# Expert stage of a gated cross-attention and MoE block: 64 experts of 96 slots against 48 tiles of 128 slots, with five scatter targets in DRAM

## The chip, the cores and the metric

The kernel runs on one core of one Trainium2 chip. The metric is the device time of one execution in microseconds; the median of three runs is given, and beside it the profile of one execution. A core has TensorE (matmuls, PE; its weight loads are listed apart as PEld), VectorE (DVE), ScalarE (ACT), GpSimd (POOL) and SyncE (SP, which here only issues transfers). A queue of transfers belongs to the engine that issues them (SPq, ACTq, POOLq); all queues are served by the same 16 DMA engines.

## The reference, cut to what matters

The block takes 16 sequences of 128 rows and 256 columns, 2048 tokens in all. It adds a cross-attention, and then a mixture of experts: 64 experts, six chosen for each token, 96 slots for each expert; every token beyond the 96th of an expert lands in its last slot, where only the last one written counts.

```
x = x + tanh(g_xattn) * xattn(layernorm(x), ctx)
logits = xn @ gate_weight.T; scores = softmax(logits)
topk_w, topk_i = top_k(scores kept in the 3 best groups, 6)
slot = expert * 96 + min(position in expert, 95)
buf = zeros(64 * 96, 256).at[slot].set(xn[tok])
g, u = buf @ Wg.T, buf @ Wu.T              # 176 columns for each expert
out = (silu(g) * u) @ Wd.T
y = sum over the 6 slots of a token of out[slot] * topk_w
x = x + tanh(g_ffn) * (y + shared(xn))     # shared: 352 columns
```

## The kernel before

All engines run a program written out by hand; semaphores order them. Everything is float32, but for the routing.

**Attention and routing** take eight steps, two sequences each (`step(r, h, par)` on each engine). In a step DVE normalises the rows into `xn2` (`norm2`, L1059), and SP saves them to `xn_rows` in DRAM (`saves`, L290), with the routing weights beside them (L297). There is one `xn2` buffer, so `norm2` of a step waits until the save of the step before has landed (`xn_saved`). DVE works out which token is in which slot; `slot_tables` turns this into two tables of row numbers, `gidx` for gathers and `sidx` for scatters. A shared expert (`shared_up`, `late_up`, `shared_down`) is computed on the way.

**SP's queue** begins with the loads of x, then the fills with zeros (L259, L262) of `even_rows`, `third_rows` and the pads behind the tables, then the experts' weights. `load_weights(g)` loads a group of two experts (1056 KB) into a ring of 12 groups; it waits until group g-2 has landed, and for g of 12 and over until the experts that used the place are done (`o_done`). The saves of `xn2` are issued on this queue, between groups: the first save follows group 3.

**The expert stage** runs over 64 experts, one after the other. POOL gathers the 96 rows of an expert with an indirect DMA (`gather`, L1540), six experts ahead. PE turns them (`turn_rows`, L582: two transposes), multiplies them by the two up projections (`up`: 8 matmuls, the weights stationary, 96 columns moving), ACT and DVE form silu(g) * u (L898, L1407), and PE multiplies by the down projection (`down`: 2 matmuls, the activations stationary, 256 columns of weights moving). One float32 matmul shows as two records on PE and two on PEld, a transpose as one of each. PE's order is `turn_rows(e+1)`, `up(e)`, `down(e-1)`. ACT scales the result by the slot's weight into `outs` (`take_out`, L909) and POOL adds it to one of three targets in DRAM with an indirect DMA that accumulates (`add_up`, L1548). Expert e goes to target e mod 3, and waits until the scatter of e-3 has landed. The third target is the output itself, which holds x and the shared expert's part from saves during the steps (`save_y`).

**The tail.** When the scatters have landed, SP reads the two other targets back (L321), PE has put the contributions of the crowded last slots into PSUM (`ov_done`), DVE adds the three (L1478, L1481), and POOL adds the sum to the output in four transfers that accumulate (L1575).

## Time and profile before

| what | value |
|---|---|
| median of 3 runs | 437.4 us (434.9 to 438.97) |
| the profiled execution | 439.52 us |
| its span on the core | 437.8 us |
| PE busy | 342.1 us, 78% |
| DVE busy | 215.8 us, 49% |
| POOL busy | 176.3 us, 40% |
| moved by DMA | 70.50 MB |

The span runs from the first to the last instruction of the profiled execution. Shares of busy time are means over stages with different limits: the steps take the first 200 us or so, the expert stage the next 205, the tail the last 30. The granted clock is TensorE's, as a share of 2.4 GHz.

### The profile page before, as it was taken

Reading aid. Unit: us, or ns where it says so; the run is one execution under the profiler, and the core shown is the slowest. Engines: PE = TensorE matmul, PEld = TensorE weight load, DVE = VectorE, ACT = ScalarE, POOL = GpSimd, SP = SyncE. Lnnn points to the kernel's source line nnn. Section 1 sums busy time; section 2 is a strip of 40 time slices with the busy share of each in tenths; the row PEclk is TensorE's granted clock in tenths of the full one; section 3 lists DMA queues with packets and bytes.
Section 4 is the critical chain, followed back from the end, with each engine's and each line's share of the span. In section 5 each row is a group of like instructions: output and inputs, shape, how many; then the busy total and the mean of one; then the engine's idle time right before and its main releaser. Section 6 shows DMA issues by size and latency. Waiting matters only on the chain.

```text
span 437.8 us, 8616 instructions
## 1 busy us (share of the span) xinstructions
PE 342.1 (78%) x2589; PEld 286.3 (65%) x2589; DVE 215.8 (49%) x879; ACT 155.8 (36%) x464; POOL 176.3 (40%) x173
## 2 busy tenths in 40 slices
PE   2779598998999796998987888777968897878600
PEld 1667486876887674886866676666856775767400
DVE  5656568789588888344764111211111211157390
ACT  2566355675466311111423223322323423223000
POOL 3000011010100111022577777776777777776231
PEclk9999979999899999899999899998999999989855
DMA  8798948447100111012598999898899444444797
GB/s 296 285 337 226 266 111 263 125 131 224 58 25 6 49 31 32 25 41 81 142 261 221 250 259 259 215 231 240 216 253 255 76 77 72 73 71 57 178 298 125
DMA packets 36265, 70.50 MB, mean 161 GB/s; under 512 B 6221, under 2 KB 23401, under 8 KB 36231
## 3 DMA queue, kind: packets, MB, share of 16 engines
q1 hardware_dynamic: 21851, 50.56, 37.0%
q0 software_dynamic: 12352, 16.26, 21.2%
q10 hardware_dynamic: 2028, 3.25, 2.3%
q8 instruction: 19, 0.31, 0.3%
q14 instruction: 15, 0.12, 0.1%
HBM read 52.26 MB, written 17.78 MB: 160 GB/s over the span
## 4 chain that ended last, share of the span: by engine, by line
PE 22%; issue 16%; DMA 8%; DVE 7%; POOL 7%; another core or an unknown queue 3%; ACT 2%; SPq 1%; DVEq 0%; ACTq 0%; POOLq 0%
PE bank L347 20%; DMA ctx_sb<-xn_rows,gidx 3%; PE bank L582 2%; DMA w_ring<-third_rows 2%; POOL result L1548 2%; POOL even_rows L1548 2%; DMA qk_sb<-xn_rows,gidx 2%; SPq L321 1%; DMA v_sb<-xn_rows,gidx 1%; POOL third_rows L1548 1%; POOL ctx_sb L1540 1%; DVE hi_hot L1188 1%; DMA even_rows<-x_all,sidx 1%; ACT pt_sb L898 1%
## 5 line engine op out<-in xcount | busy, mean ns | idle before, releaser
L347 PE MATMUL bank<-p_sb,w_ring 128*88 128x96 f32 x1024 | 97.6, 249 | 0.6 <-issue 0.6
L347 PEld LDWEIGHTS bank<-p_sb,w_ring 128*88 128x88 f32 x1024 | 92.0, 160 | 0.9 <-issue 0.8
L1407 DVE TENSOR_TENSOR pt_sb<-pt_sb,bank 88x192 f32<-88x192 f32 x64 | 22.4, 350 | 135.1 <-ACT pt_sb L898 76.4
L1529 POOL TENSOR_SCALAR zeros<-zeros,token 128x256 f16<-128x256 f16 x16 | 14.7, 928 | 155.4 <-DVE zeros L1197 155.4
L347 PE MATMUL bank<-d_ring,pt_sb 88*96 88x256 f32 x256 | 68.7, 392 | 9.5 <-DVE pt_sb L1407 9.5
L898 ACT ACTIVATE pt_sb<-bank 88x192 f32<-88x192 f32 x64 | 20.9, 327 | 94.2 <-PE bank L347 49.7
L347 PEld LDWEIGHTS bank<-d_ring,pt_sb 88*96 88x96 f32 x256 | 37.7, 167 | 19.2 <-DVE pt_sb L1407 11.7
L1548 POOL DMA_INDIRECT even_rows<-x_all,sidx x22 | 31.7, 1439 | 13.3 <-issue 4.9
L893 ACT ACTIVATE p_sb<-bank 128x192 f32<-128x192 f32 x64 | 21.1, 329 | 42.6 <-PE bank L582 22.9
L1548 POOL DMA_INDIRECT third_rows<-x_all,sidx x21 | 30.1, 1435 | 11.1 <-issue 4.0
L1548 POOL DMA_INDIRECT result<-x_all,sidx x21 | 30.2, 1436 | 10.5 <-issue 4.3
L1540 POOL DMA_INDIRECT qk_sb<-xn_rows,gidx x24 | 22.7, 947 | 24.9 <-DVE sidx L1361 17.9
L909 ACT ACTIVATE x_all<-bank,slot_w 96x256 f32<-96x256 f32 x64 | 29.6, 463 | 1.4 <-PE bank L347 0.7
L347 PE MATMUL bank<-xt_sb,sgu_sb 128*128 128x256 f32 (+1 forms) x96 | 24.2, 406 | 4.0 <-DVE x_all L1215 4.0
L347 PE MATMUL bank<-xt_late,sgu_sb 128*128 128x256 f32 (+1 forms) x96 | 23.4, 395 | 4.3 <-DVE act_t L1079 4.3
L347 PE MATMUL bank<-sd_sb,act_t 128*128 128x256 f32 (+1 forms) x96 | 25.5, 412 | 0.8 <-DVE x_all L1215 0.4
L1540 POOL DMA_INDIRECT ctx_sb<-xn_rows,gidx x24 | 22.4, 933 | 7.3 <-issue 5.5
L809 ACT ACTIVATE tanh_sb<-bank 128x256 f32<-128x256 f32 (+1 forms) x24 | 9.1, 384 | 41.2 <-PE bank L347 33.2
L347 PEld LDWEIGHTS bank<-xt_sb,sgu_sb 128*128 128x128 f32 (+1 forms) x96 | 17.9, 193 | 7.6 <-issue 4.4
L347 PE MATMUL bank<-qk_sb 128*128 128x256 f32 x64 | 18.4, 413 | 5.4 <-ACT p_sb L761 3.0
L347 PEld LDWEIGHTS bank<-xt_late,sgu_sb 128*128 128x128 f32 (+1 forms) x96 | 17.3, 186 | 8.0 <-issue 3.9
L347 PEld LDWEIGHTS bank<-sd_sb,act_t 128*128 128x128 f32 (+1 forms) x96 | 19.1, 207 | 3.8 <-DVE act_t L1079 0.7
(164 smaller groups left out, 593.6 us busy)
## 6 DMA issues: line engine op xcount, KB each, us to landing
w_ring<-wgu_in SPq DMA_DIRECT2D x32, 704.0 KB
d_ring<-wd_in SPq DMA_DIRECT2D x32, 352.0 KB
even_rows<-zeros SPq DMA_DIRECT2D x1, 2048.0 KB, 7.3
third_rows<-zeros SPq DMA_DIRECT2D x1, 2048.0 KB, 13.4
xn_rows<-xn SPq DMA_DIRECT2D x8, 256.0 KB, 5.0
result<-x_all SPq DMA_DIRECT2D x8, 256.0 KB, 2.2
w_ring<-even_rows SPq DMA_DIRECT2D x4, 512.0 KB, 7.0
w_ring<-third_rows SPq DMA_DIRECT2D x4, 512.0 KB, 7.9
```

Source lines behind the costliest of these rows:

```text
L321: sp.dma_start(rows_sb[:, n * q:n * (q + 1), :], d[P * n * q:P * n * (q + 1), :].rearrange("(n p) f -> p n f", p=P))\
L347: return pe.matmul(o, lhsT, rhs, start=start, stop=stop, skip_group_check=True)
L582: last = pe.transpose(t_ps[:, h * C:(h + 1) * C], rows[b % ROWS][:, h * P:(h + 1) * P], ident[0:C, 0:C])
L809: act.activation(tanh_sb[0:n, b, :], ps[m][0:n, 0:L], ACT.Tanh, scale=0.5)\
L893: act.activation(rows_t[:, b % 2, :], t_ps, ACT.Copy).then_inc(s["t_out"], 1)
L898: act.activation(silu_sb[:, b % 2, :], eg_ps[b % 2][:, 0:2 * C], ACT.Silu).then_inc(s["silu_ready"], 1)
L909: act.activation(outs[b % OUTS], o_ps[b % 2], ACT.Copy, scale=slot_w[:, b % 4:b % 4 + 1])\
L1188: last = dve.tensor_tensor(hi_hot[:, i, :].rearrange("p (k a j) -> p k a j", k=BLKS, a=HI), hi_key[:, i, :].rearrange("p (k a j) -> p k a ...
L1407: dve.tensor_tensor(act_tt[:, b % 2, :], silu_sb[:, b % 2, :], eg_ps[b % 2][:, 2 * C:4 * C], ALU.mult)\
L1529: last = pool.tensor_scalar(lo_hot[:, i, :], lo_hot[:, i, :], token1[:, at:at + 1], None, ALU.mult)
L1540: pool.indirect_dma_start(rows[e % ROWS], None, xn_dram, bass.IndirectOffsetOnAxis(ap=gidx[:, e:e + 1], axis=0))\
L1548: pool.indirect_dma_start(targets[e % 3], bass.IndirectOffsetOnAxis(ap=sidx[:, e:e + 1], axis=0), outs[e % OUTS], None, compute_op=ALU.add)\
```

## The change

The slots of four experts (384) are cut into three tiles of 128 slots, 48 tiles in all. Gathers, the transposes of the gathered rows, the scaling and the scatters are done by tile; `up` and `down` are still done by expert, on 96 columns of a window of six turned tiles. `down` now holds the weights stationary, in four matmuls of 96 moving columns, and its result is turned: DVE copies it out of PSUM (`take_ot`), and PE turns it back by tile (`turn_out`, two transposes). DVE forms the slot weights of three tiles at once (`slot_weights`), and copies the last slots (`keep_lasts`), which PE turns at the end; they no longer go through DRAM.

The scatters go to `acc_rows`, which holds five targets; expert e uses target e mod 5, so that a tile waits only for the scatter three tiles before. The output is no target any more: the saves of x during the steps are gone, x stays in SBUF (`outs` takes other buffers). All five targets are filled with zeros at the start, on SP's queue, at the place of the old fills. At the end the five are read back (three on SP's queue, two on ACT's); DVE adds four of them to x in SBUF in passes of eight, PE adds the fifth in PSUM, and SP writes the result with plain transfers. Token t is now kept at place (t mod 128) * 16 + t // 128 of the tables in DRAM, so that a partition's rows lie together.

```diff
+EB_TILES = EB * C // P
+TILES = E * C // P
+TARGETS = 5
+FILL_BY = 4
+TR = T + P
-AHEAD = 6
-ROWS = 8
-OUTS = 8
+AHEAD = 7
+ROW_BLKS = 3
+ROWS = ROW_BLKS * EB_TILES
+TURNED = 6
+OUTS = 4
+FILL = TR * L // P // FILL_BY
...
+            for k in range(TARGETS):
+                sp.dma_start(acc_dram.rearrange("(p a) f -> p (a f)", p=P)[:, k * FILL_BY * FILL:(k + 1) * FILL_BY * FILL]
+                             .rearrange("p (a f) -> p a f", a=FILL_BY), zero4).then_inc(s["fills_in"], 16)
+            sp.dma_start(xn_dram[T:TR, :], fill_zeros[:, 0:XW]).then_inc(s["fills_in"], 16)
...
+            read_back(sp, 4, TILES - 4)
+            read_back(sp, 0, TILES - 3)
+            read_back(sp, 2, TILES - 1)
+            for q in range(QUARTERS):
+                sp.wait_ge(s["sum_ready"], PAIRS // QUARTERS * (q + 1))
+                sp.dma_start(out_to[:, n * q:n * (q + 1), :], x_all[:, n * q:n * (q + 1), :]).then_inc(s["result_out"], 16)
...
+            def down(e):
+                at = e % (RING * GE) * DW
+                pe.wait_ge(s["at_out"], e + 1)
+                wait(pe, s["ot_out"], e - 1)
+                for h in range(H2):
+                    for m in range(2):
+                        last = mm(ot_ps[e % 2][:, h * C:(h + 1) * C],
+                                  d_ring[:, at + m * L + h * P:at + m * L + (h + 1) * P],
+                                  act_tt[:, e % 2, m * C:(m + 1) * C], start=m == 0, stop=m == 1)
+                last.then_inc(s["o_done"], 1)
+            def turn_out(t):
+                pe.wait_ge(s["ot_out"], last_expert(t) + 1)
+                wait(pe, s["o_ready"], t - 1)
+                for h in range(H2):
+                    last = pe.transpose(o_ps[t % 2][:, h * P:(h + 1) * P],
+                                        turned[t // EB_TILES % 2][:, h, P * (t % EB_TILES):P * (t % EB_TILES + 1)],
+                                        ident[:, :])
+                last.then_inc(s["turned_out"], 1)
...
+            for e in range(1, E):
+                multiply(e)
+                take_ot(e - 1)
+                if e % EB == 0:
+                    keep_lasts(e // EB - 1)
+                    slot_weights(e // EB)
+                if e % 3 == 2 and e // 3 < N:
+                    weight_parts(e // 3)
...
+            for r in range(PAIRS):
+                dve.wait_ge(s[f"back4_{r * QUARTERS // PAIRS}"], 16)
+                dve.tensor_tensor(pair(x_all, r), pair(x_all, r), pair(back[4], r), ALU.add).then_inc(s["added4"], 1)
...
+            for r in range(PAIRS):
+                dve.wait_ge(s[f"back3_{r * QUARTERS // PAIRS}"], 16)
+                dve.tensor_tensor(pair(x_all, r), pair(x_all, r), pair(back[3], r), ALU.add).then_inc(s["added3"], 1)
+                dve.wait_ge(s["ov_done"], r + 1)
+                dve.tensor_tensor(pair(x_all, r), pair(x_all, r), sum_ps[r][:, :], ALU.add).then_inc(s["sum_ready"], 1)
...
+            def add_up(t):
+                pool.wait_ge(s["o_ready"], t + 1)
+                if t > 2:
+                    pool.wait_ge(s[f"acc_in{(t - 3) % OUTS}"], 16 * ((t - 3) // OUTS + 1))
+                pool.indirect_dma_start(acc_dram, bass.IndirectOffsetOnAxis(ap=sidx[:, t:t + 1], axis=0),
+                                        outs[t % OUTS], None, compute_op=ALU.add)\
+                    .then_inc(s[f"acc_in{t % OUTS}"], 16)
```

SP's queue behind the loads of x, before. The first four groups of weights and the first save of `xn2` (L290) stand behind the fills.

```order
5 L259 DMA even_rows<-zeros 1024x1x512
6 L259 DMA third_rows<-zeros 1024x1x512
7 L262 DMA xn_rows<-zeros 96x320
8 L262 DMA even_rows<-zeros 96x256
9 L262 DMA third_rows<-zeros 96x256
10 L262 DMA result<-zeros 96x256
11 L276 DMA w_ring<-wgu_in 128x1408
12 L277 DMA d_ring<-wd_in 88x1024
...
19 L290 DMA xn_rows<-xn 128x2x256
```

The same place of the queue with the change.

```order
5 L295 DMA acc_rows<-w_ring 128x4x1088 x5
6 L297 DMA xn_rows<-w_ring 128x320
7 L311 DMA w_ring<-wgu_in 128x1408
8 L312 DMA d_ring<-wd_in 88x1024
...
15 L318 DMA xn_rows<-xn 128x2x256
```

The five fills write 4 * 1088 * 4 bytes in each of 128 partitions, 2.23 MB each, 11.14 MB in all, and the pad of `xn_rows` 0.16 MB. Before it was 2 * 2.10 MB and pads of 0.42 MB: 4.61 MB. What follows them is in the same order as before, up to the saves of x, which are gone.

PE in the middle of the expert stage, before: an expert is two transposes of gathered rows, `up` and `down`.

```order
209 L582 MATMUL bank<-ident,qk_sb 128x96 x2
210 L347 MATMUL bank<-p_sb,w_ring 88x96 x8
211 L347 MATMUL bank<-d_ring,pt_sb 96x256 x2
212 L582 MATMUL bank<-ident,qk_sb 128x96 x2
213 L347 MATMUL bank<-p_sb,w_ring 88x96 x8
214 L347 MATMUL bank<-d_ring,pt_sb 96x256 x2
```

PE with the change, over four experts (L609 is `turn_rows`, L643 `turn_out`; in L375, `hi_hot,w_ring` is `up` and `xn,d_ring` is `down`).

```order
219 L609 MATMUL bank<-ident,ctx_sb 128x128 x2
220 L375 MATMUL bank<-hi_hot,w_ring 88x96 x8
221 L375 MATMUL bank<-xn,d_ring 128x96 x4
222 L643 MATMUL bank<-ident,act_t 128x128 x2
223 L375 MATMUL bank<-hi_hot,w_ring 88x96 x8
224 L375 MATMUL bank<-xn,d_ring 128x96 x4
225 L609 MATMUL bank<-ident,p_sb 128x128 x2
226 L375 MATMUL bank<-hi_hot,w_ring 88x96 x8
227 L375 MATMUL bank<-xn,d_ring 128x96 x4
228 L643 MATMUL bank<-ident,pt_sb 128x128 x2
229 L609 MATMUL bank<-ident,p_sb 128x128 x2
```

A `down` has four matmuls where it had two, and two transposes of results stand behind it wherever a tile is full: 96 transposes of rows and 96 of results over the stage, where there were 128 of rows.

DVE at the end of its program, before: these pairs of adds stand eight times, one pair for two sequences.

```order
547 L1478 TENSOR_TENSOR w_ring<-w_ring 128x512
548 L1481 TENSOR_TENSOR w_ring<-w_ring,bank0 128x512
549 L1478 TENSOR_TENSOR w_ring<-w_ring 128x512
550 L1481 TENSOR_TENSOR w_ring<-w_ring,bank1 128x512
551 L1478 TENSOR_TENSOR w_ring<-w_ring 128x512
```

DVE at the same place with the change; the last two stand eight times in turn.

```order
657 L1521 TENSOR_TENSOR x_all<-x_all,w_ring 128x512 x8
658 L1525 TENSOR_TENSOR x_all<-x_all,w_ring 128x512 x8
659 L1529 TENSOR_TENSOR x_all<-x_all,w_ring 128x512 x8
660 L1533 TENSOR_TENSOR x_all<-x_all,w_ring 128x512
661 L1536 TENSOR_TENSOR x_all<-x_all,bank2 128x512
```

The adds go from 16 to 40, and the first three passes must be through before the first quarter of the result can be complete.

## Rows read from the trace of the kernel before

**Rows 1.** Windows: the expert stage (us, busy by engine, PEclk, DMA share, GB/s)

```profile
210.00:404.00 194.00, 160.08 (x1370) 135.23 (x1368) 55.61 (x208) 61.65 (x186) 142.33 (x120) 0.97 0.75 181
```

**Rows 2.** Timeline of POOL: the first scatter, and a steady stretch

```profile
213.26 1.52 POOL L1548 DMA_INDIRECT even_rows<-x_all,sidx  x1 [3.16 <-ACT x_all L909]
...
323.24 0.94 POOL L1540 DMA_INDIRECT qk_sb<-xn_rows,gidx  x1 [0.30 <-DVE slot_w L1416]
324.48 1.44 POOL L1548 DMA_INDIRECT third_rows<-x_all,sidx  x1 [0.30 <-issue]
```

**Rows 3.** The scatters' line L1548: what POOL waited for (us, times)

```profile
  ACT x_all L909: 11.5, 11
  DVE slot_w L1416: 10.1, 9
  DMA even_rows<-x_all,sidx: 0.3, 1
```

**Rows 4.** Timeline of PE: one expert that waits for nothing

```profile
329.95 0.33 PE L582 MATMUL bank<-ident,qk_sb 96*128 96x96 f32 x2
...
330.12 1.49 PE L347 MATMUL bank<-p_sb,w_ring 128*88 128x96 f32 x16
...
331.44 1.03 PE L347 MATMUL bank<-d_ring,pt_sb 88*96 88x256 f32 x4
...
332.31 0.33 PE L582 MATMUL bank<-ident,qk_sb 96*128 96x96 f32 x2
```

**Rows 5.** Timeline of PE: 128 stationary columns, in a step

```profile
103.11 0.60 PE L383 MATMUL bank<-ident,p_sb 128*128 128x128 f32 x4
103.54 0.61 PE L347 MATMUL bank<-qkv_sb,ctx_sb 128*128 128x128 f32 x4
...
107.44 1.10 PE L347 MATMUL bank<-gate_sb,xt_sb 128*128 128x64 f32 x8 [0.25 <-ACT xt_sb L787]
```

**Rows 6.** Timeline of SP's queue: first fill, group 2, first save

```profile
14.36 0.61 SPq L259 DMA_DIRECT2D even_rows<-zeros  x1
...
36.21 0.36 SPq L276 DMA_DIRECT2D w_ring<-wgu_in  x1
...
42.54 0.40 SPq L290 DMA_DIRECT2D xn_rows<-xn  x1
```

**Rows 7.** Timeline of DVE: the second pair's norm

```profile
52.12 0.81 DVE L1059 TENSOR_SCALAR xn<-x_all,mv,guess 128x256 f32 x2 [4.45 <-DMA xn_rows<-xn]
```

**Rows 8.** Windows of the start (columns as in rows 1)

```profile
5.00:10.00 5.00, 1.47 (x4) 1.18 (x4) 4.28 (x28) 2.48 (x5) 0.53 (x3) 1.00 1.02 397
...
20.00:25.00 5.00, 3.96 (x26) 2.81 (x24) 1.74 (x5) 3.85 (x13) 0.00 (x0) 1.00 1.02 351
```

**Rows 9.** Timeline of PE: `down` of expert 0, and of the last

```profile
209.66 1.10 PE L347 MATMUL bank<-d_ring,pt_sb 88*96 88x256 f32 x4 [0.25 <-DVE pt_sb L1407]
...
401.58 2.11 PE L347 MATMUL bank<-d_ring,pt_sb 88*96 88x256 f32 x8
```

**Rows 10.** Timeline of POOL and SP's queue: last scatter, reads, last write

```profile
406.16 1.43 POOL L1548 DMA_INDIRECT even_rows<-x_all,sidx  x1 [0.30 <-issue]
...
427.12 1.28 POOL L1575 DMA_DIRECT2D result<-w_ring  x1 [1.73 <-DVE w_ring L1481]
...
409.47 0.42 SPq L321 DMA_DIRECT2D w_ring<-even_rows  x1
```

**Rows 11.** Windows of the tail: reading back, accumulating writes

```profile
417.00:419.00 2.00, 0.00 (x0) 0.00 (x0) 1.64 (x4) 0.00 (x0) 0.00 (x0) 0.74 1.09 348
...
427.00:429.00 2.00, 0.00 (x0) 0.00 (x0) 0.00 (x0) 0.00 (x0) 1.28 (x1) 0.50 1.24 196
```

**Rows 12.** Groups by line: DVE's adds; and transfers to landing

```profile
L1478 DVE TENSOR_TENSOR w_ring<-w_ring 128x512 f32<-128x512 f32 x8 | 5.5, 688 | 7.1 <-DMA w_ring<-third_rows 7.1
...
result<-x_all SPq DMA_DIRECT2D x8, 256.0 KB, 2.2
```

**Rows 13.** Chain that ended last: a gather's transfer (start, us)

```profile
320.26 6.67 DMA qk_sb<-xn_rows,gidx
```

More of the change, by code:

```diff
@@ L235, in build @@
[L235 to L242 removed]
+            rows_in0 rows_in1 rows_in2 rows_in3 rows_in4 rows_in5 rows_in6 rows_in7 rows_in8
@@ L695, in _ @@
-            for t in range(N):
-                pe.wait_ge(s["w_parts_ready"], t + 1)
-                if t // 2 == 6:
-                    pe.wait_ge(s["o_ready"], E)
-                for k, part in enumerate((high_mid, high_mid, high_low)):
-                    if k == 0 and t in early:
-                        continue
-                    last = mm(bank[t // 2][:, t % 2 * L:(t % 2 + 1) * L], part[:, t * P:(t + 1) * P],
-                              last_parts[:, k, :], start=k == 0, stop=k == 2)
-                last.then_inc(s["ov_done"], 1)
+            turn_rows(1)
@@ new lines, in _ @@
+            take_rows(0)
+            act.wait_ge(s["ht_done"], N)
+            silu(0)
+            take_rows(1)
+            act.wait_ge(s["qk_done"], N)
+            act.wait_ge(s["h_done"], N)
+            for e in range(1, E):
+                if e < E - 1 and last_tile(e + 1) > last_tile(e):
+                    take_rows(last_tile(e + 1))
+                silu(e)
+                t = last_tile(e - 2) if e > 1 else 0
+                if last_expert(t) == e - 2:
+                    take_out(t)
+                elif t > 0 and last_expert(t - 1) == e - 2:
+                    take_out(t - 1)
@@ L1530, in weigh_hots @@
                 last.then_inc(s["hot_ready"], 1)
[L1532 to L1533 removed]
+            for r in range(2, PAIRS + 1):
                 weigh_hots(r)
[L1536 to L1542 removed]
@@ L1544, in add_up @@
[L1544 to L1551 removed]
+            pool.wait_ge(s["qk_done"], N)
+            pool.wait_ge(s["v_done"], N)
```

544 lines of the change are left out of this document (285 added, 259 removed).

## Prediction, made blind

> **What bounds the kernel now.** I read the windows first. In the expert stage, 210 to 404 us, PE is busy 160.08 of 194 us, POOL 142.33, DVE and ACT about 60, and the DMA engines 0.75 [rows 1]. None is full, so the next view is POOL's timeline. There gather and scatter alternate with 0.30 us between them: 0.94 + 0.30 + 1.44 + 0.30 = 2.98 us for an expert, 191 us for 64, near to the stage's length. The gaps are the engine's own, not a wait [rows 2]. The scatters' own view shows how much POOL waited beyond that: 11.5 + 10.1 us for ACT and DVE, which is mostly where the rows of a gather had come late, and 0.3 us for an earlier scatter [rows 3]. So POOL's number of instructions sets the pace. PE is second: where an expert waits for nothing, it takes 2.36 us from one turning of rows to the next (329.95 to 332.31), 151 us for 64 [rows 4].
>
> Ahead of the stage the steps are bound by PE and DVE in turn, but at one place by a transfer. SP issues the fills from 14.36 us; group 2 of the weights must wait until group 0, behind the fills, has landed (36.21), group 3 waits in the same way for group 1, and only then goes the first save of `xn2` at 42.54 [rows 6]. DVE's second norm waits for that save, 4.45 us, until 52.12 [rows 7]. While the fills run the DMA engines are full, at 351 GB/s [rows 8]. So what stands ahead of this save on SP's queue is on the path.
>
> **The change: the expert stage.** POOL has 48 gathers and 48 scatters for 64 of each, but of 128 rows for 96. No row shows another number of rows. If a DMA costs the same whatever its rows, a tile takes 2.98 us; if it goes with the rows, 1.25 + 0.30 + 1.92 + 0.30 = 3.77 us. I take 1.03 and 1.57 us, near the lower end, since the direct transfers at the end issue 512 rows of 1 KB in 1.28 us [rows 10]. From the first scatter on there are 48 scatters and 41 gathers: 48 * 1.87 + 41 * 1.33 = 144 us, with 137 and 170 at the ends. Before it was 194 us from 213.26 to 407.6.
>
> The Trainium skill (DMA: Bandwidth & Descriptors, Anatomy of one DMA) says of descriptor generation that many descriptors can be emitted before the incremental cost shows up; by it the lower end holds, 137 us, and the sum stays as it is, for PE is then the bound either way.
>
> PE loses nothing but gains transposes. From 209.66 us (`down` of expert 0 [rows 9]) there are 62 `up` left, each 331.44 - 330.12 = 1.32 us: 82 us. `down` was four records with 256 moving columns, 332.31 - 331.44 = 0.87 us [rows 4]. Now it is eight records with 96 moving columns and 128 stationary ones. Rows with 128 stationary columns show what that costs: eight with only 64 moving columns are 1.10 us on PE, of which 0.17 us is the last one's way out (as with `up`, 1.49 us long at a pace of 1.32), so 0.93 us [rows 5]. The loads set that pace, not the moving columns. `up` has 88 stationary columns and goes at 0.083 us a record; at that pace `down` would be 0.66 us. I take 0.94, from the row with the same load: 64 of them are 60 us. Four transposes of 128 columns follow each other in 103.54 - 103.11 = 0.43 us [rows 5], 0.22 us for a tile; 45 tiles of rows and 48 of results are left: 20.5 us. Sum 163 us. TensorE's granted clock was 0.97 of full in this stage [rows 1], which adds 5 us; PE will be denser, so I don't take less. For rows that come late I add 4 us: the DMA engines have the same bytes to move in less time, and DVE's `slot_weights` wants three tiles landed before the next `multiply`. PE then ends its last `down` 172 us after 209.66, where it took 194.0 (to 401.58 + 2.11 [rows 9]): **22 us saved**, between 30 and 10.
>
> The Trainium skill (TensorE: Matmul & The Clock Gate, LDWEIGHTS) says that a weight load takes its number of columns divided by 1.2 in ns, whatever the contraction. By it eight loads of 128 columns are an estimated 0.85 us, 5.5 us less in all than by the row, and the sum would be 439.5. The rule too speaks against stationary weights here; of the trace, the transposes agree with it and the eight matmuls don't, so it is a rival below.
>
> DVE gets `take_ot` beside `multiply`, of the same size; it was busy 55.61 of 194 us [rows 1], and twice that still fits in 172. It is hidden by PE's 2.6 us for an expert; if that cover went, it would be POOL's pace that shows. The five targets change no wait that exists: three scatters were in flight before, and POOL waited 0.3 us for them [rows 3]. The old saves of x and the wait for them are gone; they held the seventh gather, but not PE, so I count nothing.
>
> **The start.** Fills and pads grow from 4.61 to 11.30 MB and stand ahead of group 0, and so of the first save. 6.69 MB at 345 GB/s (351 in the fullest window of the fills [rows 8], a little less for what ACT's queue loads beside them) are **19.4 us**. DVE is already waiting when the save lands, so nothing hides it: the wait of 4.45 us becomes some 24 us, PE and ACT stand behind it, and every later step moves by as much. The lower end takes all the fills at the fastest window, 397 GB/s [rows 8]: 11.3 / 0.397 - 4.61 / 0.345 = 15 us. The upper takes the pace of this queue alone: 4.61 + 1.08 MB from 14.36 to 36.21 [rows 6], 0.26 MB/us, 25 us. The few more small instructions of the tables on DVE cost 0.5 us, most of them beside PE's shared expert.
>
> **The tail.** Before, from the end of `down` (403.7) to the span's end at 437.8, it took 34.1 us. The last scatter began at 406.16, its landing freed SP at 409.47 [rows 10], 4.19 MB were read at 348 GB/s, and the result was added by POOL at 196 GB/s [rows 11], the last quarter from 427.12 [rows 10], of which the writes that were queued before it are a part. I put the end after the last landing at 3 us. Now, counted from PE's last `down`: target 4 is read from about 0, target 0 from 3, target 1 from 5, targets 2 and 3 from 6.6 us (two turnings, ACT, and two scatters come first). 10.5 MB at 348 GB/s are 30 us: all is in at 31. DVE has 40 adds of 0.69 us [rows 12], 27.6 us, and can't begin before 3.6. The first pass ends at 9, the second waits for target 0 until 20 (it shares the engines with target 1), the third ends at 26, and the last 16 adds at 37, which is later than the last transfer. PE's eight matmuls for target 2 lie beside these. The last quarter of the result is written plainly: 0.5 us to issue and 3 to land, since half of its size took 2.2 [rows 12], then the 3 us of the end: 43.5 us. **9.4 us more**, between 5 and 13.
>
> **The sum.** 437.8 + 19.4 + 0.5 - 22 + 9.4 = 445.1 us of span. The profiled execution took 439.52 us, 1.7 more than its span, and is 2.1 above the median of the runs shown; so the median should be 444.7, say **445 us**, 1.7% slower. About 1% (4.4 us) is what a measurement of this kernel can tell from no change.
>
> **Rivals.**
> *Loads hide beside moving columns* (ends faster). `down` goes at the 0.083 us a record of `up`, since its 96 moving columns cover the load, and the contraction of 88 rows helps. 64 * 0.28 = 18 us less, and 2 more if the clock stays full: 425 to 429. It decides once a record of `down` takes less than 0.095 us, which makes the median drop under 433. For it: `up` is as short in moving columns. Against it: the eight with 64 moving columns at 0.117 [rows 5]. Chance 0.13.
> *Loads at the transposes' pace*: 128 stationary columns at 0.43 / 4 = 0.108 us [rows 5], so 0.86 us for a `down`; 64 * 0.08 = 5 us less, 440, within 1%. Chance 0.10.
> *The start costs 15 us*: the fills run at 397 GB/s, 440 to 441, within 1%. For it: their rows of 4.3 KB are longer than the old 2 KB. Chance 0.09.
> *POOL goes with its rows*: 170 us after the first scatter, plus the 12 us that it waited before. Its last scatter then begins 180 us after the first, 393 + 20 against 404.6 in my account, 9 us more: 454. For it: 1.44 against 0.94 us shows that a row's work counts for something. Against it: the direct transfers [rows 10]. Chance 0.14.
> *Rows come late*: gathers of 1280-byte rows share full DMA engines, and DVE stands still in `slot_weights` with `multiply` behind it, then PE. A gather is issued seven tiles ahead; it decides from a landing of some 12 us, where the chain shows 6.67 us [rows 13]. 8 to 12 us more: 455. Chance 0.08.
> *The targets do nothing*: that the five targets shorten no wait is in my forecast already, by the 0.3 us.
>
> **How the numbers follow.** The forecast has 0.46, with a range of its own of 441 to 450. Faster by over 1% (under 433): the first rival, and a little for the next two together, 0.15. Within 1% (433 to 441.8): the rest of those two and the low edge of the forecast, 0.23. Slower: 0.62. The range from 432 to 457 leaves out most of the first rival and the ends where start, tail and POOL all cost their most.
>
> **What would show it.** Right: DVE's second norm waits over 15 us for `xn_rows<-xn`, and PE starts the expert stage near 222 to 230 us. PEld of `down` near 0.95 us for eight records, PE busy over 90% from there to its last `down`, some 172 us later. POOL's scatters near 1.6 us, with idle time that ends by ACT. In the tail DVE busy nearly throughout its last 17 us, and about 43 us from PE's last `down` to the end. Wrong: a norm that waits under 10 us, a `down` of 0.7 us, scatters of 1.9 us with gaps of 0.30, or gathers that land 12 us after their issue.

## The result, and the profile after

The kernel with the change took 423.1 us (median of 4 runs, 419.9 to 426.7), the kernel before, run beside it, 438.2 (434.9 to 439.1). The ratio is 0.967, with a 95% interval of 0.961 to 0.974: **3.3% faster**, where 445 us was predicted. Medians, here and below, are of all executions of a kernel, while ratios and intervals leave out those more than 1.5% slower than its fastest. The profiled execution has a span of 422.8 us, against 437.8.

The span is compared in three pieces, cut at PE's first and last `down`: the start up to `down(0)`, the expert stage, and the tail.

| piece | before | after | measured | predicted |
|---|---|---|---|---|
| start, to `down(0)` | 209.7 | 222.1 | +12.4 | +19.9 |
| expert stage | 194.0 | 159.9 | -34.1 | -22 |
| tail, from the last `down` | 34.1 | 40.8 | +6.7 | +9.4 |
| sum | 437.8 | 422.8 | -15.0 | +7.3 |

Each term has the sign that was predicted, and each missed on the same side, by 7.5, 12.1 and 2.7 us.

**The start.** DVE's timeline at the second pair's norm, and SP's queue, after (start, us, engine, line, instruction, and in brackets the wait before it); they answer to [rows 6, 7].

```profile
65.06 0.83 DVE L1075 TENSOR_SCALAR xn<-x_all,mv,guess 128x256 f32 x2 [15.56 <-DMA xn_rows<-xn]
```

```profile
14.30 11.15 SPq L295 DMA_DIRECT2D acc_rows<-w_ring  x5
...
50.86 0.34 SPq L311 DMA_DIRECT2D w_ring<-wgu_in  x1
...
56.21 0.38 SPq L318 DMA_DIRECT2D xn_rows<-xn  x1
```

The first save goes at 56.21 where it went at 42.54, and the wait for it grew from 4.45 to 15.56 us. The windows of the fills (us; busy us of PE, PEld, DVE, ACT, POOL; granted clock; DMA share; GB/s) show why it did not grow to 24: these are well over the 351 and 345 GB/s that the sum took [rows 8].

```profile
20.00:25.00 5.00, 4.13 (x29) 3.48 (x28) 1.52 (x6) 3.60 (x10) 0.85 (x4) 1.00 1.03 396
...
30.00:35.00 5.00, 3.81 (x28) 3.47 (x28) 3.18 (x15) 3.16 (x12) 0.00 (x0) 1.00 1.01 416
```

**The expert stage.** The window over it, after; it answers to [rows 1].

```profile
222.05:381.97 159.92, 159.46 (x1690) 159.06 (x1688) 74.49 (x267) 55.84 (x154) 110.75 (x86) 1.00 0.83 215
```

PE is busy 159.46 of 159.92 us, and the granted clock is 1.00, where it was 0.97 with PE busy 160.08 of 194 us. PE has more to do than before (at a clock of 1.00 the old work is 151.97 us, in b_half_scatters below), but it does not wait any more. PE's timeline over one expert and a bit more (L609 turns rows, L643 results; in L375 `hi_hot,w_ring` is `up` and `xn,d_ring` is `down`) answers to [rows 4].

```profile
299.02 0.38 PE L609 MATMUL bank<-ident,p_sb 128*128 128x128 f32 x2
299.23 1.48 PE L375 MATMUL bank<-hi_hot,w_ring 128*88 128x96 f32 x16
300.55 1.06 PE L375 MATMUL bank<-xn,d_ring 88*128 88x96 f32 x8
301.45 0.38 PE L643 MATMUL bank<-ident,act_t 128*128 128x128 f32 x2
```

From start to start, `up` takes 1.32 us, `down` 0.90, a turning 0.21. POOL's timeline beside it, which answers to [rows 2]:

```profile
299.31 0.99 POOL L1632 DMA_INDIRECT qk_sb<-xn_rows,gidx  x1 [0.30 <-issue]
300.61 1.58 POOL L1641 DMA_INDIRECT acc_rows<-x1n,sidx  x1 [0.30 <-issue]
302.49 0.99 POOL L1632 DMA_INDIRECT qk_sb<-xn_rows,gidx  x1 [0.31 <-PE bank L609]
304.49 1.58 POOL L1641 DMA_INDIRECT acc_rows<-v_sb,sidx  x1 [1.01 <-DMA acc_rows<-v_sb,sidx]
```

A tile costs POOL 0.99 + 0.30 + 1.58 + 0.30 = 3.17 us, and PE 1.33 experts of 2.22 us and two turnings, 3.38. POOL is close behind PE. The last row shows it waiting for the scatter three tiles back; there were three such waits, 3.4 us in all, and none reached PE.

**The tail.** A window of the reads, and DVE's last adds and the writes (timeline); they answer to [rows 10 to 12].

```profile
399.00:401.00 2.00, 0.00 (x0) 0.00 (x0) 1.29 (x2) 0.00 (x0) 0.00 (x0) 0.50 1.01 414
```

```profile
409.10 0.69 DVE L1533 TENSOR_TENSOR x_all<-x_all,w_ring 128x512 f32<-128x512 f32 x1 [1.24 <-DMA w_ring<-acc_rows]
...
411.87 8.27 SPq L342 DMA_DIRECT2D result<-x_all  x4
...
419.09 0.69 DVE L1536 TENSOR_TENSOR x_all<-x_all,bank 128x512 f32<-128x512 f32 x1
```

The reads go at 414 GB/s, where 348 was taken. DVE's last 16 adds begin when the first quarter of target 3 lands, and end at 419.8, 3.0 us before the span does. The last bytes of the result move before 422.0, 0.8 us before the end; in the kernel before, whose last transfers accumulate on POOL's queue, next to nothing moved after 434.0, 3.8 us before the end (windows, after and before):

```profile
421.00:422.00 1.00, 0.00 (x0) 0.00 (x0) 0.00 (x0) 0.00 (x0) 0.00 (x0) 0.50 0.91 365
422.00:422.80 0.80, 0.00 (x0) 0.00 (x0) 0.00 (x0) 0.00 (x0) 0.00 (x0) 0.50 0.00 0
```

```profile
434.00:437.80 3.80, 0.00 (x0) 0.00 (x0) 0.00 (x0) 0.00 (x0) 0.00 (x0) 0.50 0.00 0
```

### The profile page after: what moved, and what is told of

The parts are those of the page before. It is cut to its first block, busy times and chain, and to the rows that moved or that the text cites. A ratio compares the mean times of both kernels' runs of the same rounds, so it can differ in the third digit from the quotient of the medians.

```text
span 422.8 us, 9173 instructions
## 1 busy us (share of the span) xinstructions
PE 353.9 (84%) x2935; PEld 316.2 (75%) x2935; DVE 247.6 (59%) x956; ACT 150.4 (36%) x432; POOL 157.7 (37%) x199
## 4 chain that ended last, share of the span: by engine, by line
PE 46%; DVE 7%; issue 5%; DMA 5%; POOL 2%; SPq 0%; ACT 0%; DVEq 0%; POOLq 0%
PE bank L375 41%; DMA w_ring<-acc_rows 3%; PE bank L609 2%; PE bank L643 2%; DMA acc_rows<-x1n,sidx 2%; POOL acc_rows L1641 2%; DVE hi_hot L1204 1%; DVE x_all L1533 1%; SPq L270 0%; DVE xn L1075 0%; DVE x_all L1231 0%; DVE zeros L1213 0%; DVE act_t L1095 0%; DVE newest L1173 0%; DVE guess L993 0%
## 5 line engine op out<-in xcount | busy, mean ns | idle before, releaser
L375 PE MATMUL bank<-hi_hot,w_ring 128*88 128x96 f32 x1024 | 95.0, 246 | 0.9 <-issue 0.6
L375 PEld LDWEIGHTS bank<-hi_hot,w_ring 128*88 128x88 f32 x1024 | 90.8, 157 | 1.3 <-issue 0.8
L1614 POOL TENSOR_SCALAR zeros<-zeros,token 128x256 f16<-128x256 f16 x16 | 14.6, 926 | 151.3 <-DVE zeros L1213 151.3
L375 PE MATMUL bank<-xn,d_ring 88*128 88x96 f32 x512 | 67.6, 275 | 0.0
L1438 DVE TENSOR_TENSOR xn<-h_sb,bank 88x192 f32<-88x192 f32 x64 | 22.3, 349 | 73.3 <-ACT h_sb L931 59.2
L375 PEld LDWEIGHTS bank<-xn,d_ring 88*128 88x128 f32 x512 | 62.2, 192 | 0.0
L1641 POOL DMA_INDIRECT acc_rows<-x1n,sidx x24 | 37.9, 1579 | 26.4 <-ACT x1n L939 17.8
L1641 POOL DMA_INDIRECT acc_rows<-v_sb,sidx x24 | 40.0, 1665 | 16.5 <-issue 7.1
L931 ACT ACTIVATE h_sb<-bank 88x192 f32<-88x192 f32 x64 | 20.9, 327 | 65.1 <-PE bank L375 57.6
L375 PE MATMUL bank<-xt_sb,sgu_sb 128*128 128x256 f32 (+1 forms) x96 | 24.2, 406 | 4.0 <-DVE x_all L1231 4.0
L375 PE MATMUL bank<-xt_late,sgu_sb 128*128 128x256 f32 (+1 forms) x96 | 23.7, 398 | 4.3 <-DVE act_t L1095 4.3
L375 PE MATMUL bank<-sd_sb,act_t 128*128 128x256 f32 (+1 forms) x96 | 25.0, 406 | 0.8 <-DVE x_all L1231 0.4
L843 ACT ACTIVATE tanh_sb<-bank 128x256 f32<-128x256 f32 (+1 forms) x24 | 9.1, 384 | 41.5 <-PE bank L375 33.5
L375 PEld LDWEIGHTS bank<-xt_sb,sgu_sb 128*128 128x128 f32 (+1 forms) x96 | 17.9, 193 | 7.6 <-issue 4.4
L375 PE MATMUL bank<-qk_sb 128*128 128x256 f32 x64 | 19.4, 429 | 5.0 <-ACT p_sb L795 2.6
L375 PEld LDWEIGHTS bank<-xt_late,sgu_sb 128*128 128x128 f32 (+1 forms) x96 | 17.5, 187 | 8.1 <-issue 4.0
L925 ACT ACTIVATE hi_hot<-bank 128x256 f32<-128x256 f32 x48 | 18.1, 379 | 12.4 <-PE bank L609 10.7
L375 PEld LDWEIGHTS bank<-sd_sb,act_t 128*128 128x128 f32 (+1 forms) x96 | 18.9, 205 | 3.7 <-DVE act_t L1095 0.7
L375 PE MATMUL bank<-v_sb,pt_sb 128*128 128x128 f32 x128 | 17.7, 281 | 2.4 <-ACT pt_sb L803 2.4
L375 PE MATMUL bank<-w_ring,ident 128*128 128x512 f32 x16 | 9.9, 790 | 11.5 <-DMA w_ring<-acc_rows 11.5
```

The source lines that it names most:

```text
L375: return pe.matmul(o, lhsT, rhs, start=start, stop=stop, skip_group_check=True)
L843: act.activation(tanh_sb[0:n, b, :], ps[m][0:n, 0:L], ACT.Tanh, scale=0.5)\
L925: act.activation(rows_t[:, :, to:to + P], t_ps[t % 2].rearrange("p (h f) -> p h f", h=H2), ACT.Copy)\
L931: act.activation(silu_sb[:, e % 2, :], eg_ps[e % 2][:, 0:2 * C], ACT.Silu).then_inc(s["silu_ready"], 1)
L1438: dve.tensor_tensor(act_tt[:, e % 2, :], silu_sb[:, e % 2, :], eg_ps[e % 2][:, 2 * C:4 * C], ALU.mult)\
L1614: last = pool.tensor_scalar(lo_hot[:, i, :], lo_hot[:, i, :], token1[:, at:at + 1], None, ALU.mult)
```

## The experiments

The kernels ran in four groups, each on one chip, beside the kernel before. That kernel had a median of 441.4, 438.3, 431.0 and 441.6 us on the four chips (the groups of the table, in this order), so ratios from different chips compare to about 2% only. The pieces of the span, cut as above, are steadier. "d0" is when `down(0)` begins, "clock" the granted clock of the stage. The runs named half or small leave out a part of the block's sums or of the weights and so don't compute the block; only their time is read.

| kernel | median us | ratio (95%) | d0 | stage | clock | tail |
|---|---|---|---|---|---|---|
| before | | 1 | 209.7 | 194.0 | 0.97 | 34.1 |
| after | 423.1 | 0.967 (0.961-0.974) | 222.1 | 159.9 | 1.00 | 40.8 |
| *chip 1:* a_fills_late | 410.0 | 0.931 (0.923-0.939) | 203.8 | 159.3 | 1.00 | 40.6 |
| a_fill_2k | 428.7 (1 run) | | 225.5 | 159.4 | 1.00 | 42.0 |
| a_wait2 | 437.2 | 0.989 (0.985-0.993) | 222.3 | 174.0 | 0.98 | 39.9 |
| a_half_down | 417.1 | | 220.4 | 151.3 | 1.00 | 41.2 |
| *chip 2:* b_small_loads | 436.3 | 0.997 (0.992-1.002) | 206.2 | 189.0 | 0.98 | 34.1 |
| b_pool_more | 438.3 | 0.998 (0.995-1.002) | 210.9 | 194.3 | 0.95 | 33.9 |
| a_pool_more | 423.5 | 0.966 (0.962-0.970) | 222.4 | 159.2 | 1.00 | 40.9 |
| a_late_tail | 406.1 | 0.928 (0.925-0.930) | 207.6 | 159.2 | 1.00 | 41.5 |
| *chip 3:* b_half_scatters | 411.3 | 0.956 (0.948-0.964) | 205.8 | 163.8 | 1.00 | 33.0 |
| a_small_loads | 424.7 (1 run) | | 222.7 | 159.2 | 1.00 | 41.0 |
| a_half_small | 407.2 (1 run) | | 223.4 | 141.4 | 1.00 | 40.7 |
| a_back_1k | 428.7 | 0.998 (0.993-1.004) | 221.2 | 159.2 | 1.00 | 43.2 |
| *chip 4:* after_base | 425.3 | 0.964 (0.957-0.972) | | | | |
| a_back_1k_2 | 430.2 | 0.974 (0.966-0.982) | | | | |
| a_fills_late_2 | 411.8 | 0.933 (0.924-0.942) | 205.3 | 159.3 | 1.00 | 41.3 |
| a_late_tail_2 | 406.8 | 0.925 (0.918-0.931) | 205.0 | 159.5 | 1.00 | 40.5 |

In the profiled executions of after_base and a_back_1k_2 PE waited for rows that came late, and their stages took 163.6 and 166.5 us; their rows of the table are left open, and `down(0)` and tail of both are given where they bear on a reading.

### What the fills cost the start

The fills are issued behind the saves of steps 1 to 4 (a_fills_late):

```diff
+                if 1 <= r <= 4:
+                    for k in ((0, 1), (2,), (3,), (4,))[r - 1]:
+                        fill(k)
```

> The kernel with the change, but SP issues the five fills and the pad of xn_rows behind the saves of steps 1 to 4 (two fills, one, one, one) and no longer ahead of the weights. Theory (the fills ahead of the first save cost the start all of DVE's wait of 15.56 us at its second norm): that wait falls to under 1 us, PE's down of expert 0 comes 12 to 16 us earlier than 222.05, stage and tail stay as long as they were, and the time is 408 to 411 us against 423. Rival (the fills only move the stall: behind the first saves they hold the later saves and the weights' groups, and with them DVE's norms of steps 2 to 5): waits of 2 to 5 us turn up at several norms, and the time is 415 to 423 us.

The theory held: no norm of DVE waits over 1 us, and `down(0)` came 18.3 us earlier, more than the 12 to 16 expected.

```profile
64.88 0.80 DVE L1079 TENSOR_SCALAR xn<-x_all,mv,guess 128x256 f32 x2 [0.94 <-DMA xn_rows<-xn]
```

(That is the third pair's norm, the longest such wait; the second's, which waited 15.56 us, begins at 48.11 with a wait of 0.26.) The same 11.1 MB now run beside the steps and hold nothing. The size was measured again beside the unedited kernel, on one chip:

> The kernel with the change, unedited, as the base for the three others on the same chip. If chips treat both kernels alike, the ratio to the kernel before is 0.967 again, within 0.006. If they differ, it lies between 0.96 and 0.99, and ratios of different calls can't be compared to 1%.

> The kernel with the change, with the fills behind the saves of steps 1 to 4, as before, now beside the unedited kernel. Theory (the fills cost the start 15.6 us of wait and some 3 us of lower clock behind it, as the two profiles show: down of expert 0 at 222.05 and 203.77): 15 to 19 us less than the unedited kernel, a ratio lower by 0.035 to 0.043. Rival (a part was the other chip's): 10 to 14 us less.

The medians differ by 13.6 us and the ratios by 0.031 (0.933 and 0.964), which is the rival's range and not the theory's. The profiles say more: `down(0)` begins at 220.4 to 223.4 us in seven profiles with the fills ahead, at 203.8 to 207.6 in four with the fills behind, 222.1 and 205.4 on average, 16.6 us apart (after_base and a_back_1k_2, at 224.8 and 224.2, would make it 17.2). Both hold within the intervals; 14 to 17 us is what the fills cost. And since the late fills bring `down(0)` under the 209.7 of the kernel before, whose own fills cost it 4.45 us, the whole of the start's loss is theirs.

Whether the length of the rows set the rate (a_fill_2k):

```diff
-FILL_BY = 4
+FILL_BY = 8
```

> The kernel with the change, but each partition's fill of 17.4 KB is written as eight rows of 2.2 KB instead of four of 4.3 KB; the bytes are the same. Theory (the row's length sets the rate: 4.3 KB rows went at 397 to 409 GB/s, where the 2 KB rows of the kernel before went at 351): 11.3 MB take 32 us instead of 28, DVE's second norm waits 19 to 23 us instead of 15.6, and the time is 426 to 431 us. Rival (the rate is the engines' own, and the kernel before was slower there because ACT's loads and SP's first loads of x lay beside it): the norm waits 15 to 16.5 us, and the time stays at 421 to 425.

```profile
67.91 0.83 DVE L1075 TENSOR_SCALAR xn<-x_all,mv,guess 128x256 f32 x2 [20.37 <-DMA xn_rows<-xn]
```

The wait was 20.37 us, where the same start has 15.56, 17.46 and 16.68 us in the profiles of after, a_wait2 and a_half_down: 3.8 us more than their mean. But the nine profiles with this start have 15.6 to 19.4 us, 17.2 on average, so one wait alone says little. What scatters less is when SP issues the first save: at 56.2 to 57.6 us in the nine (56.8 on average), and here at 59.5, 2.7 us later:

```profile
59.52 0.39 SPq L318 DMA_DIRECT2D xn_rows<-xn  x1
```

Its slices of 10.7 us moved 378 and 376 GB/s, where after's moved 397 and 409. So the row's length moves the rate, as the theory has it. It isn't all: with rows of 2.2 KB the fills still go faster than the 340 to 351 GB/s of the kernel before, and why is open. By 376 GB/s the start's term would have been 11.3 / 0.376 - 4.61 / 0.345 = 16.7 us, a wait of 21.1, for 20.37 measured in this one run.

### What set the pace before

Two edits of the kernel before. In b_small_loads each group of weights from the 13th on loads an eighth of its columns; in b_half_scatters only experts of even number are scattered:

```diff
+                gu_n, d_n = (GE * GU, GE * DW) if fixed else (GE * GU // 8, GE * DW // 8)
```

```diff
             def add_up(e):
+                if e % 2:
+                    return
```

> The kernel before, but each group of weights from the 13th on loads only the first eighth of its columns, so that the DMA engines are nearly free during the expert stage; the multiplications are the same, and experts 24 and on multiply with what the ring held otherwise. Theory (POOL's number of instructions set the pace before, 2.98 us for an expert, as the prediction had it): the stage, 194.0 us from PE's down of expert 0 to its last down, stays at 188 to 193 us, PE's waits for gathered rows (15.8 us in 10 places) turn into waits for DVE or ACT, and the ratio to the kernel before is 0.985 to 1. Rival (full DMA engines made the gathers late, and these the stage): the stage falls to 160 to 180 us, towards PE's 151, and the ratio is 0.92 to 0.97.

> The kernel before, but only the experts of even number are added to the targets: 32 scatters instead of 64, all else the same. It leaves out the contributions of half the experts. Theory (POOL's gathers and scatters set the pace of the stage before): POOL needs 2 x 1.24 + 1.74 = 4.22 us for two experts, PE 4.72, so PE becomes the bound, and the stage falls from 194.0 to 152 to 168 us (PE's 151 and what late rows cost), ratio 0.90 to 0.94. Rival (the pace before came from something else, the chain PE, ACT, DVE or the full DMA engines): stage 180 to 194 us, ratio 0.97 to 1.

With the DMA engines half empty (share 0.49) the stage was 189.0 us, still at the pace of POOL's row of instructions, whose gathers begin 2.98 us apart (at 302.71, 305.69, 308.67 and 311.65 us); PE's waits for gathered rows were gone, and in their place stood 24.8 us of waits for DVE's `multiply`, 25 times. With half the scatters the stage fell to 163.8 us:

```profile
205.84:369.68 163.84, 151.97 (x1370) 130.92 (x1370) 55.74 (x209) 63.39 (x187) 98.50 (x89) 1.00 0.74 196
```

PE is busy 151.97 us, the 151 of the prediction, and the other 11.7 us are its waits for gathered rows, all before 322 us, where the DMA share is 0.95. So POOL did set the pace before, and fewer instructions on POOL free the stage down to PE's own work and the late rows. The changed kernel has no such waits. It gathers further ahead, seven tiles of 128 rows for six of 96; no run takes that back alone, so how its share and that of the fewer instructions divide the 34 us isn't shown.

A second test of the same claim said nothing. One memset of a column stood ahead of each scatter, in both kernels:

```diff
             def add_up(e):
+                pool.memset(more[:, e:e + 1], 0.0)
```

> The kernel before, with one small extra instruction on POOL ahead of each scatter (a memset of one column in a buffer that nothing reads): 64 more instructions in the expert stage. Theory (POOL sets the pace): each costs its own time plus a gap of some 0.06 to 0.30 us, all of it seen in the stage, 64 times 0.1 to 0.4: 6 to 26 us longer, ratio 1.015 to 1.06, and about 1.5 times as much as the same instruction costs in the changed kernel per tile or more. Rival (POOL has slack before, PE and late rows bound): under 3 us.

> The kernel with the change, with the same small extra instruction on POOL ahead of each scatter, 48 of them. Theory (PE bounds, POOL stands 0.16 us a tile behind it and waits for ACT in most tiles): where the extra instruction costs under 0.16 us, nothing is seen; at 0.3 us it costs 48 times 0.14 = 7 us at most. Expected 0 to 4 us, 423 to 427 against 423, ratio to the kernel before 0.967 to 0.977. Rival (POOL bounds here too): the same cost per instruction as in the kernel before, 5 to 20 us, ratio 0.98 to 1.01.

Neither kernel grew. POOL's timeline in b_pool_more shows that this is no slack:

```profile
324.07 0.94 POOL L1541 DMA_INDIRECT qk_sb<-xn_rows,gidx  x1 [0.30 <-issue]
325.01 0.12 POOL L1546 MEMSET more<- 128x1 f32 x1
325.32 1.45 POOL L1550 DMA_INDIRECT third_rows<-x_all,sidx  x1 [0.19 <-issue]
```

The memset's 0.12 us lies inside the gap of 0.30 us, of which 0.19 is left; an expert takes 3.00 us with it, 2.98 without. The dose was too small to price anything.

### What bounds the stage after

a_half_down leaves out the second half of `down`'s sum, and with it 4 of 8 records for each expert; a_small_loads and a_half_small load an eighth of the weights from the 13th group on, the first with the whole `down`:

```diff
-                    for m in range(2):
+                    for m in range(1):
```

> The kernel with the change, but down does only the first of its two terms (activations 0 to 87): two matmuls of 96 columns instead of four for each expert. It leaves out half of the down projection's sum. Theory (PE bounds the stage, and POOL stands 0.16 us a tile behind it, 3.17 against 3.33 us): PE has 64 times 0.45 = 28 us less to do, POOL takes over at 3.17 us a tile, the stage is 152 to 155 us instead of 159.9, and the time 415 to 419. PE is then idle between experts, and the granted clock, 1.00 all through the stage so far, falls under 0.98 in some of its windows. Rival (POOL has slack enough and PE alone bounds): stage 132 to 140 us, time 395 to 403. Second rival (the clock falls with more work and not with idle time): the clock stays at 1.00 in every window.

> The kernel with the change, but each group of weights from the 13th on loads only the first eighth of its columns; the multiplications are the same, and experts 24 and on multiply with what the ring held otherwise. Theory (PE alone bounds the stage, and the full DMA engines cost it nothing): the stage, 159.9 us, stays at 158 to 160, and POOL's 3.4 us of waits for earlier scatters go. Rival (contention with the weights costs the stage something, late landings of scatters above all): 153 to 157 us.

> Both edits together: down does only the first of its two terms, as in the experiment on it, and the groups of weights from the 13th on load an eighth of their columns. With the full loads, half the down projection made the stage 151.3 us, and PE waited 11.3 us for gathered rows. Theory (full DMA engines, which made the gathers late, took PE's place as the bound there): PE's waits for rows go, and the stage is 138 to 145 us, with POOL (48 scatters of 1.88 us and 41 gathers of 1.29 us, 143 us) as the next bound. Rival (POOL was the bound already, and the late rows came from gathers issued late): 149 to 152 us.

Half of `down` shortened the stage by 8.6 us, to 151.3, and not by the 28 that PE lost. The size was near the 152 to 155 expected, but for another reason: POOL did not take over, it waited too. PE's timeline shows what did:

```profile
291.36 0.61 PE L375 MATMUL bank<-xn,d_ring 88*128 88x96 f32 x4
291.81 0.38 PE L643 MATMUL bank<-ident,act_t 128*128 128x128 f32 x2
293.55 0.44 PE L609 MATMUL bank<-ident,p_sb 128*128 128x128 f32 x2 [1.36 <-DMA p_sb<-xn_rows,gidx]
```

It waited 11.3 us for gathered rows, ten times, while the DMA engines were full (share 1.01 from 290 to 300 us). With small loads beside it the stage was 141.4 us, and POOL's timeline is then a closed row:

```profile
317.72 1.58 POOL L1642 DMA_INDIRECT acc_rows<-x1n,sidx  x1 [0.30 <-issue]
319.60 0.99 POOL L1633 DMA_INDIRECT qk_sb<-xn_rows,gidx  x1 [0.31 <-issue]
320.89 1.58 POOL L1642 DMA_INDIRECT acc_rows<-x1n,sidx  x1 [0.30 <-issue]
```

That is the 143 us of POOL in the expectation, and with POOL's row closed, the 7.8 us that PE still waits for rows would come from gathers issued late. With the whole `down`, small loads changed nothing (159.2), though POOL's waits for earlier scatters went, as expected. So in the changed kernel PE bounds; the full DMA engines stand some 8 us behind it, POOL some 18.

My expectation on the clock was wrong, and the second rival right: a_half_down left PE idle for 16 us of its stage, in 17 waits of up to 1.53 us, and the clock stayed 1.00 in every window of 2 us.

### What the targets are worth

a_wait2 lets a scatter wait for that of two tiles back:

```diff
-                if t > 2:
-                    pool.wait_ge(s[f"acc_in{(t - 3) % OUTS}"], 16 * ((t - 3) // OUTS + 1))
+                if t > 1:
+                    pool.wait_ge(s[f"acc_in{(t - 2) % OUTS}"], 16 * ((t - 2) // OUTS + 1))
```

> The kernel with the change, but the scatter of tile t waits for that of t-2 instead of t-3, so that two scatters are in flight. Theory (a scatter's landing takes longer than two tiles of 3.3 us while the queues are loaded; POOL waited for the one three tiles back 3.4 us in all): POOL waits 1 to 3 us in most tiles, becomes the bound of the stage, and the time is 15 to 40 us longer, 438 to 463. Rival (the targets do little, as the prediction took from 0.3 us of waits in the kernel before): 0 to 3 us longer, 423 to 426.

The stage grew by 14.1 us, and the ratio by 0.022, some 10 us, against after's on another chip: less than the 15 to 40 of the theory, far more than the 0 to 3 of the rival. POOL waited 15.9 us for earlier scatters, seven times, and not in most tiles. What it cost came from what stands behind the waiting scatter in POOL's queue, the next gather: PE waited 9.5 us for gathered rows, twice over 2 us, and at those two places the clock fell.

```profile
261.21 0.69 PE L609 MATMUL bank<-ident,ctx_sb 128*128 128x128 f32 x2 [2.30 <-DMA ctx_sb<-xn_rows,gidx]
```

```profile
260.00:265.00 5.00, 3.79 (x27) 3.79 (x28) 0.34 (x1) 1.19 (x3) 2.59 (x3) 0.66 0.93 269
```

The run keeps all five targets, so it shows the waits of a kernel with fewer, and not what that kernel would save in fills and reads, 2.2 and 2.1 MB for each target. The fill need cost nothing, as above.

### The tail

a_back_1k cuts each read of a quarter in two, of every second token, so that its rows are 1 KB long:

```diff
+                for i in range(2):
+                    eng.dma_start(back[k][:, n * q + i:n * (q + 1):2, :],
```

> The kernel with the change, but the targets are read back in rows of 1 KB instead of 4 KB: each transfer of a quarter is cut in two, of which one takes every second token, 40 transfers instead of 20, the same 10.5 MB. Theory (the row's length sets the rate, 348 GB/s with 1 KB before, 411 with 4 KB after): the reads take 30 us instead of 25.5, the first quarter of target 3 lands 4 to 5 us later, and the time is 427 to 429 us, ratio 0.975 to 0.98. Rival (1 KB rows go at the same rate in plain reads, and the kernel before read slower for another reason): 423 to 425, ratio 0.966 to 0.970.

> The kernel with the change, with the targets read back in rows of 1 KB, as before, now beside the unedited kernel. Theory (the rate alone): 2 to 5 us more than the unedited kernel on the same chip, a ratio higher by 0.005 to 0.012. Rival (1 KB rows cost something that the profile doesn't show): 10 us more or over, a ratio higher by 0.023 or more.

```profile
399.00:401.00 2.00, 0.00 (x0) 0.00 (x0) 0.29 (x2) 0.00 (x0) 0.00 (x0) 0.50 1.10 348
```

The rate is 348 GB/s again, to the digit, as the theory has it. The first quarter of target 3 lands 29.1 us after PE's last `down` for 27.1, not 4 to 5 us later as expected, and the tail is 43.2 us for 40.8 (43.5 for 41.4 in the profiles on chip 4). Beside the unedited kernel it cost 4.9 us by the medians, with intervals that overlap (0.974 and 0.964). That the tail of 43.2 is near the 43.5 predicted with that rate is luck, for DVE's last add ends 40.2 us after PE's last `down`, where the sum had 37:

```profile
419.84 0.69 DVE L1537 TENSOR_TENSOR x_all<-x_all,bank 128x512 f32<-128x512 f32 x1
```

The ratio of 0.998 on chip 3 does not say otherwise: the kernel before took 431 us there, and a_small_loads, whose pieces are those of the unedited kernel, 424.7, a ratio of 0.985. Why the kernel before is faster on that chip was not found.

a_late_tail has the late fills and lets PE add target 0 in PSUM too:

```diff
+            for r in range(PAIRS):
+                pe.wait_ge(s[f"back0_{r * QUARTERS // PAIRS}"], 16)
+                mm(sum_ps[r][:, :], ident[:, :], back[0][:, 2 * r:2 * r + 2, :].rearrange("p n f -> p (n f)"),
+                   start=False, stop=False)
```

> The kernel with the change, with the fills behind the saves of steps 1 to 4 as in the first experiment, and one more edit: in the tail PE adds target 0 in PSUM too, by eight more multiplications with the identity, and DVE's passes are target 4, target 1, the sum in PSUM, target 3, so that 8 adds instead of 16 are left when the first quarter of target 3 has landed (409.10 us after the change), and 32 instead of 40 in all. Theory (DVE's adds bound the last 11 us of the tail): the eight adds and the last write end 4 to 5.5 us earlier, 404 to 406 against the 410 of fills behind the saves alone, ratio 0.918 to 0.922. Rival (PE's multiplications, at a granted clock of 0.5 to 0.76 there, or the landing of target 3 hold the end instead): 408 to 412, ratio 0.925 to 0.935.

> The fills behind the saves and the tail with target 0 added by PE, as before, beside the kernel with the late fills alone. Theory from the profile of the first run (the tail took 41.5 us from PE's last down, against 40.6 and 40.8 without the edit: DVE's sum waited for PE's multiplications at half clock): the same as the late fills alone within 2 us. Rival (the profiled execution was a slow one, and the edit gives what was expected first): 3 to 5 us less.

DVE has 8 adds less, but the tails are 41.5 and 40.5 us, where the late fills alone have 40.6 and 41.3. The timeline of the first run:

```profile
399.42 0.69 DVE L1537 TENSOR_TENSOR x_all<-x_all,bank 128x512 f32<-128x512 f32 x1 [0.17 <-PE bank L379]
400.02 4.90 DVE L1541 TENSOR_TENSOR x_all<-x_all,w_ring 128x512 f32<-128x512 f32 x8
```

The sum's adds wait for PE, and PE for the last quarter of target 2; the eight adds of target 3 stand behind them. The landing of the reads, not DVE, holds the end: the rival. On chip 4, which has both, the median is 5.0 us under that of the late fills and the ratio 0.008 lower, some 3.7 us; but the intervals overlap, and the tails differ by 0.7 us only, so it stays open between the theory (within 2 us) and its rival (3 to 5). The kernel is still the fastest of all, 0.925 of the kernel before.

## Why the prediction was wrong

**The step that failed is the stage's sum, "Sum 163 us ... which adds 5 us; PE will be denser, so I don't take less ... For rows that come late I add 4 us".** What bounds, what takes over and which parts count were all right. The sum of PE's work is 62 * 1.32 + 64 * 0.90 + 93 * 0.22 = 159.9 us, and the stage took 159.9, and 159.2 to 159.5 in eight other runs. Of the 12.1 us missed:
- 5 us are the clock. I carried over the mean of a stage in which PE waited, and argued that more work would not mend it. The three falls before stand behind waits; in the nine profiles whose stage took 159.2 to 159.9 us, PE was idle under 0.6 us in all, and the clock was 1.00. Whoever removes waits may give that clock back.
- 4 us are the late rows. The cover was there: seven tiles ahead, PE waited for none. It is thin, as a_half_down shows, where waits of up to 1.53 us come back as soon as PE is faster.
- 3 us are `down`, 0.90 for 0.94 us (2.6 us), and rounding. The rival *Loads at the transposes' pace* had it at 0.86. The Trainium skill (TensorE: Matmul & The Clock Gate, LDWEIGHTS) gives an estimated 0.85 us for the eight loads; the trace lies between that and the row of the same load.

**The start: "6.69 MB at 345 GB/s".** The place and the wait were right, the rate was not: the fills went at 396 to 416 GB/s with rows of 4.3 KB. That was the rival *The start costs 15 us*, whose 397 GB/s stood in my own rows, of other transfers. I took the row of the old 2 KB fills. By the measured rate, 403 GB/s (the mean of 397 and 409 above), the term is 11.3 / 0.403 - 4.61 / 0.345 = 14.7 us, and group 2 of the weights, which waits behind the fills, is issued 14.65 us later than before (50.86 for 36.21). So 4.7 of the 7.5 us missed are the rate; a_fill_2k gives back 2.7 of them, for the length of the rows. Another 1.5 us are the scatter of single profiles (by the averages the start grew by 13.9 us, not 12.4), and some 1.3 us stay open.

**The tail: "0.5 us to issue and 3 to land ... then the 3 us of the end".** Here the time of DVE's adds was right, by two errors that cancel. The reads went at 411 GB/s and not at 348, the same mistake with 1 KB rows for 4 KB. And the sum let the last 16 adds follow the third pass at 26 us, while they wait for the first quarter of target 3, which lands at 27.1, and at 29.1 with 1 KB rows. So they end at 37.8 us, where the sum had 37. What was missed is the end behind them: 6.5 us in the sum, 3.0 measured. The 3 us after the last landing were taken from the kernel before, which ends in accumulating writes on POOL's queue and stands still for 3.8 us; behind SP's plain write it is 0.8 us. a_back_1k puts 2.4 us back at the reads, but it does not restore the sum's own account.

**Right as predicted.** POOL's pace before [rows 2]; its instructions with 128 rows, 1.03 and 1.57 us predicted, 0.99 and 1.58 measured, so that *POOL goes with its rows* falls; DVE hidden behind PE. That "the five targets change no wait that exists" held as far as PE goes: POOL waited 3.4 us for earlier scatters for the 0.3 before [rows 3], and none reached PE. But those 0.3 us said nothing of two in flight, which cost 14 us in the stage. One sum is off without effect: POOL's lower end is 48 * 1.74 + 41 * 1.24 = 134 us, not 137.

The range of 432 to 457 failed twice. The terms' own lower bounds (15.5, -30, +5) sum to a span of 428.3 us, which the range left out, as if the three could not fail together; all three leaned on rates and a clock taken from the old conditions. And start and stage, with +12.4 and -34.1, came out under their bounds: the stage's left out that all the waits could go; the start's is off by less than single profiles scatter (`down(0)` begins at 208.2 on average in the four profiles of kernels with the old start, 13.9 us ahead of the 222.1 above).

## What to carry to other kernels

When a change removes the waits of the busiest engine, price its stage by the sum of its instructions at the pace of a stretch without waits, and take the old stage's clock and lateness as things that may go with the waits. Take a transfer's rate from a row with the same row length. Take what follows the last landing from a kernel that ends with the same kind of write. And ask of every large transfer at the start what stands behind it in its queue: moving five fills behind four small saves was worth as much here as the whole rest of the change.

## What the runs showed of the hardware

- Rows of 1 KB were read at 348 GB/s, of 4 KB at 404 to 422, with the same DMA share of 1.0 to 1.1. Fills in rows of 2.2 KB went at 376 to 378, of 4.3 KB at 397 to 409, in slices of 10.7 us.
- From the last bytes moved to the end of the span it took 3.8 us behind POOL's accumulating writes (before), and 0.8 us behind SP's plain ones (after).
- An indirect gather took POOL 0.94 us for 96 rows and 0.99 for 128, a scatter that adds 1.44 and 1.58.
- A gap of 0.30 us stands between POOL's indirect transfers, and a memset of 0.12 us fits into it at no cost.
- The granted clock fell in the stage behind some of PE's waits (2.30 and 2.16 us in a_wait2; 1.77, 3.20 and 1.98 before), yet not behind 2.45 us at 340.32 before, nor in a_half_down with 17 waits of up to 1.53. In b_small_loads it fell to 0.87 and 0.79 from 285 to 295 us, where no wait was over 1.63. What decides it was not found.
